# Joining the MLP stage and the second attention stage of a four-stage kernel into one program

## The reference, cut to what matters

```python
x = x + _layernorm(_L0_attn_ref(_layernorm(x), ...))   # attention with a running maximum
x = x + _layernorm(_L0_ffn_ref(_layernorm(x), ...))    # the MLP
x = x + _layernorm(_L1_attn_ref(_layernorm(x), ...))   # spectral attention
x = x + _layernorm(_L1_ffn_ref(_layernorm(x), ...))    # experts, one chosen per token

def _L0_ffn_ref(x, ...):                               # ternary weights, 128 -> 512 -> 512 -> 512 -> 128
    h = silu(_tlin(x, w1_w, w1_s)) * _tlin(x, w2_w, w2_s)
    h = gelu(_tlin(h, h1_w, h1_s)); h = gelu(_tlin(h, h2_w, h2_s))
    return _tlin(h, w3_w, w3_s)

def _L1_attn_ref(x, w_qkv, w_out):                     # 8 heads of 16 features
    q, k, v = split(x @ w_qkv)
    kv = cumsum(fft(k) * fft(v), axis=1)
    return ifft(kv * conj(fft(q))).real @ w_out
```

## Time and profile before

| what | value |
|---|---|
| runs, us | 1738.9, 1739.12, 1739.66 (median 1739.12) |
| the profiled execution's own time, us | 1737.36 |
| its span, first to last instruction, us | 1735.6 |
| PE busy | 1554.0 us, 90% of the span |
| DVE busy | 1288.1 us, 74% |
| ACT busy | 1164.1 us, 67% |
| POOL busy | 713.0 us, 41% |
| mean granted PE clock | 0.948 of full speed |

### The profile page before, as it was taken

How to read it: one execution, slowest core, us unless ns; L and a number is a source line. 1 busy time by engine, 2 the same in 40 slices (tenths; PEclk the granted TensorE clock), 3 DMA queues, 4 the chain that set the end, 5 groups by cost and what they waited for, 6 DMA issues and landing times. The chain is left out here.

```text
span 1735.6 us, 34433 instructions
## 1 busy us (share of the span) xinstructions
PE 1554.0 (90%) x8456; PEld 851.6 (49%) x8456; DVE 1288.1 (74%) x3545; ACT 1164.1 (67%) x2434; POOL 713.0 (41%) x1011
## 2 busy tenths in 40 slices
PE   4999999999999999999669999999949997896995
PEld 2333333333333333333247777777725655564773
DVE  4899999999999999999646666666636885323664
ACT  1588888888888888888646666667614455563663
POOL 2224433434443434333332333333314442474886
PEclk7799999999999999999879999999979998998998
DMA  4223223323222232331000000000030000444442
GB/s 124 61 78 93 82 85 94 91 75 90 82 86 86 80 98 84 108 91 45 8 7 1 1 1 0 0 0 0 1 102 1 1 1 1 137 154 130 140 136 67
DMA packets 83617, 109.24 MB, mean 63 GB/s; under 512 B 15915, under 2 KB 48945, under 8 KB 83520
## 3 DMA queue, kind: packets, MB, share of 16 engines
q1 hardware_dynamic: 77120, 91.28, 18.6%
q0 software_dynamic: 6400, 16.82, 2.7%
HBM read 63.24 MB, written 40.08 MB: 60 GB/s over the span
## 5 line engine op out<-in xcount | busy, mean ns | idle before, releaser
L838 DVE TENSOR_REDUCE bmax<-PS 128x8 f32<-128x512 f32 x1024 | 651.1, 683 | 60.0 <-PE PS L576 57.7
L688 ACT ACTIVATE EX<-PS 128x512 f32<-128x512 f32 x1024 | 564.0, 603 | 102.9 <-PE PS L587 93.6
L576 PE MATMUL PS<-KR,QR 33*128 33x512 f32 x1024 | 408.3, 468 | 37.9 <-DVE bmax L838 24.9
L587 PE MATMUL PS<-QR,KR 64*128 64x512 f32 x1024 | 395.9, 459 | 1.6 <-ACT EX L688 1.5
L576 PEld LDWEIGHTS PS<-KR,QR 33*128 33x128 f32 x1024 | 166.3, 188 | 350.8 <-DVE bmax L838 295.9
L597 PE MATMUL PS<-EX,VS 128*9 128x512 f32 x2048 | 268.6, 596 | 1.2 <-ACT EX L688 1.2
L587 PEld LDWEIGHTS PS<-QR,KR 64*128 64x128 f32 x1024 | 161.6, 185 | 11.3 <-ACT EX L688 10.2
L1030 PE MATMUL PS<-pA,wb 128*128 128x512 f32 x640 | 156.9, 401 | 0.0
L773 POOL TENSOR_TENSOR m_diff<-m_prev,m_all 128x16 f32<-128x16 f32 x64 | 14.3, 223 | 311.5 <-DVE m_all L850 311.5
L1030 PEld LDWEIGHTS PS<-pA,wb 128*128 128x128 f32 x640 | 120.1, 191 | 27.5
L1178 ACT ACTIVATE gelud<-PS,scales 128x512 f32<-128x512 f32 x128 | 88.4, 690 | 61.3 <-PE PS L1030 58.2
(11 more groups left out here) (230 smaller groups left out, 2784.4 us busy)
## 6 DMA issues: line engine op xcount, KB each, us to landing
QR<-q_scr SPq DMA_DIRECT2D x256, 64.0 KB, 2.4
KR<-k_scr SPq DMA_DIRECT2D x256, 64.0 KB, 2.3
big<-row_scr SPq DMA_DIRECT2D x72, 192.5 KB, 2.4
k_scr<-partsB SPq DMA_DIRECT2D x42, 256.0 KB, 2.9
q_scr<-partsB SPq DMA_DIRECT2D x28, 256.0 KB, 3.0
X<-in_L_attn_x SPq DMA_DIRECT2D x16, 256.0 KB, 3.0
X<-x SPq DMA_DIRECT2D x16, 256.0 KB, 2.4
xB<-in_L_attn_x SPq DMA_DIRECT2D x14, 256.0 KB, 3.3
```

The lines of the kernel that those rows point to most:

```text
L576: pe.matmul(PS[:, bank_of(i, n), :], QR[rows, i, h // 2, t * P:(t + 1) * P], KR[rows, i, h // 2, :], start=True, stop=True).then_inc(tile_ ...
L587: pe.matmul(PS[:, RING3 + bank_of(j, n), :], KR[rows, j, h // 2, kt * P:(kt + 1) * P], QR[rows, j, h // 2, :], start=True, stop=True).then ...
L688: act.activation(EX[:, n % (2 * HG), :], PS[:, RING3 + bank_of(j, n), :], ACT.Exp, scale=SCALE).then_inc(ex_set, 1)
L838: dve.tensor_reduce(bmax[:, i % 2, n, :], PS[:, bank_of(i, n), :].rearrange("p (b k) -> p b k", k=BLK), AX_X, ALU.max).then_inc(tile_max, 1)
```

## The change

The MLP's block is dissolved. Its engine programs become functions (`mlp_sync`, `mlp_tensor`, ...) that are called at the head of the second attention's block, so there is no barrier between the two.

- `run_pairs` no longer runs the drain. Each engine writes it out behind its last pair, and a part of it moves behind the first instructions of the attention: `turn` of chunks 14 and 15 behind `combine(0)` and `output(0)` on PE, `copy_xT` likewise on ACT, `x_stats` and `x_rows` of chunk 15 behind `products(0)` and `products(1)` on DVE.
- SP loads the fold matrices once the last first-layer product is done (`in_done`), into a part of the buffer `row` that lies where `pX` lay; `row` itself is used much later. The two matrices of `combine` get a buffer of their own, `mix`, and are loaded with `gate_w` and the constants after the MLP's last product (`mlp_done`). `w6_in` now counts seven transfers, `w5_in` still four.
- New waits keep banks and buffers apart: `xT3_set` before a chunk's `project`, `lnB["steps"]` before the first q products and the first `combine`, `xT3_set` before the first `output` and the first `logits`, `hi_set` before the folds, `mlp_done` before DVE's constants.
- PE's last `turn_y` stands behind the If and the Else, so the jump over the Else side now lies between `layer_out` and `turn_y` of chunk 15.

The diff without changes of indentation, cut:

```diff
@@ run_pairs
             step(PAIRS - 1, True, True)
-            step(PAIRS, False, True)
@@ end of the MLP's PE program
                 with pe.If(exact == 1):
                     run_pairs(pe, step_of(True))
+                turn_y(PAIRS - 1, 0)
+                layer_out(PAIRS - 1, 1, True)
                 with pe.Else():
                     run_pairs(pe, step_of(False))
+                turn_y(PAIRS - 1, 0)
+                layer_out(PAIRS - 1, 1, False)
+            turn_y(PAIRS - 1, 1)
+            return turn
@@ end of the MLP's POOL and ACT programs
                 run_pairs(pool, step)
+            step(PAIRS, False, True)
...
                 run_pairs(act, step)
+            copy_y(PAIRS - 1, 0)
+            copy_y(PAIRS - 1, 1)
+            return copy_xT
@@ end of the MLP's DVE program
                 run_pairs(dve, step)
+            y_stats(PAIRS - 1, 0)
+            y_rows(PAIRS - 1, 0)
+            x_stats(PAIRS - 1, 0)
+            y_stats(PAIRS - 1, 1)
+            x_rows(PAIRS - 1, 0)
+            y_rows(PAIRS - 1, 1)
+            return x_stats, x_rows
@@ buffers of the attention
+        mix = sb("mix", [P, 2, P])
+        row = sb("row", [P, 2, NT, ROW])
+        early = row[:].rearrange("p s t r -> p (s t r)")
+        wqkvT = early[:, 0:3 * P].rearrange("p (k i) -> p k i", k=3)
+        wout1 = early[:, 3 * P:4 * P]
+        turns = early[:, 4 * P:8 * P].rearrange("p (k i) -> p k i", k=4)
@@ SP
-                sp.dma_start(wqkvT[:], ...).then_inc(w5_in, 16)
-                sp.dma_start(wout1[:], io["L1_attn_w_out"]).then_inc(w5_in, 16)
-                sp.dma_start(dft[:], ...).then_inc(w5_in, 16)
-                sp.dma_start(gate_w[:], io["L1_ffn_gate_w"]).then_inc(w5_in, 16)
+                mlp_sync(sp)
+                sp.wait_ge(in_done, PAIRS * 16)
+                sp.dma_start(wqkvT, ...).then_inc(w5_in, 16)
+                sp.dma_start(wout1, io["L1_attn_w_out"]).then_inc(w5_in, 16)
+                sp.dma_start(turns[:, 0:2, :], ...).then_inc(w5_in, 16)
+                sp.dma_start(turns[:, 2:4, :], ...).then_inc(w5_in, 16)
+                sp.wait_ge(mlp_done, 2 * PAIRS)
+                sp.dma_start(mix[:], ...).then_inc(w6_in, 16)
+                sp.dma_start(gate_w[:], io["L1_ffn_gate_w"]).then_inc(w6_in, 16)
@@ PE
+                turn_x4 = mlp_tensor(pe)
                 pe.wait_ge(w5_in, 64)
+                pe.wait_ge(hi_set, PAIRS * 16)
...
                 def project(c, s):
                     xT = chunk_of(XT, c)
+                    pe.wait_ge(xT3_set, c + 1)
...
                     if late(c, 1):
                         pe.wait_ge(qq_set, c)
+                    else:
+                        pe.wait_ge(lnB["steps"], (NCH - 1) * LN_SPLIT)
...
                 def combine(c, s):
...
+                    else:
+                        pe.wait_ge(w6_in, 112)
+                        pe.wait_ge(lnB["steps"], NCH * LN_SPLIT)
...
                 run_stages(pe, NCH, [(0, project), (6, ranks), (4, turn), (1, combine), (2, output), (5, logits),
+                                     (1, lambda c, s: turn_x4(PAIRS - 1, 0) if c == 0 else None),
+                                     (2, lambda c, s: turn_x4(PAIRS - 1, 1) if c == 0 else None),
                                      (SHARED_LAG, shared)])
@@ ACT
+                copy_x4 = mlp_scalar(act)
...
-                act.wait_ge(w6_in, 80)
+                act.wait_ge(w6_in, 112)
...
+                                      (1, lambda c, s: copy_x4(PAIRS - 1, 0) if c == 0 else None),
+                                      (2, lambda c, s: copy_x4(PAIRS - 1, 1) if c == 0 else None),
@@ DVE
+                x4_stats, x4_rows = mlp_vector(dve)
+                dve.wait_ge(mlp_done, 2 * PAIRS)
                 dve.memset(ones5[:], 1.0).then_inc(const5_set, 1)
...
-                dve.wait_ge(w6_in, 80)
+                dve.wait_ge(w6_in, 112)
...
-                run_stages(dve, NCH, [(0, products), (3, residual), ...
+                run_stages(dve, NCH, [(0, products), (0, lambda c, s: x4_stats(PAIRS - 1, 1) if c == 0 else None),
+                                      (1, lambda c, s: x4_rows(PAIRS - 1, 1) if c == 0 else None), (3, residual), ...
```

More of the change, by code:

```diff
@@ L1195, in step @@
+                        turn_y(p - 1, 0)
+                        layer_out(p - 1, 1, exact)
+                    if now:
+                        layer_in(p, 1, exact)
                     if before:
-                        copy_y(p - 1, 0)
+                        turn_y(p - 1, 1)
                     if now:
-                        for n in range(2 * FB):
-                            silu(p, n)
-                            if n == FB and before:
-                                copy_y(p - 1, 1)
```

537 lines of the change are left out of this document (267 added, 270 removed).

## The result

The changed kernel took 1705.18 us, median of five runs (1703.78 to 1710.11), against 1739.12 before: a ratio of 0.9815, 95% interval 0.9802 to 0.9828. The forecast was 1716.4 with a range of 1713.0 to 1721.0. The direction was right and the time fell out of the range, on the fast side.

The account below looks back on a forecast made before the run. One chain of waits across engines, then on PE, was taken to bound the seam up to DVE's fourth `products`. 23.9 us less 1.2 gave 22.7: 1737.36 profiled becomes 1714.7, plus 1.76 gives 1716.4, range 1713.0 to 1721.0.

Parts of the forecast that it names:

- The step that failed: End of the MLP: its last product stays at 1260.13 us, as the pairs are the same code.
- clock in the folds: Seven folds after the last `turn_y`: run at the full clock, 1.7 us in place of 3.4.
- two groups of transposes on PE: Two groups of four transposes moved into the attention: 0.66 us each, about 0.6 counting, 1.2 in all, hidden by nothing.
- gain at the fourth `products`: Sum at the start of the second attention: 23.9 us less 1.2 for transposes, 22.7; v(3) ends at 1289.8 instead of 1312.46.
- The jump: PE's jump over the Else side ahead of the last `turn_y`: `turn_y` begins between 1260.9 and 1262.7, late end taken.
- a covered jump: Bound for PE's jump wholly covered by the last products in its queue: gain 23.1 us, time 1716.0.
- The constants: DVE sets its constants behind the last `y_rows`: 1.2 us, so `products(0)` starts at 1271.4.
- ids: Seven `w6_in` transfers land at 1267.7; ACT copies k and q until about 1269.8, PE needs more at 1270.4: covered.
- the clock didn't stay low: Rival: half clock persists into the attention, 7 us more per chunk; 1758 if for six chunks; chance 3%.
- the first rival: Clock falls once in the drain: folds take 3.4 us instead of 1.7, gain 20.7, time 1718.4; chance 13%.
- The rival without overlap: A wait ties the first projection to the drain's end; only pause and loads go: 12.3 us, 1726.8; chance 10%.
- a microsecond or two either way: Bound for clock holes behind 1300 us falling differently against the work: a microsecond or two.

Follow-up runs that it names:

- wb_off_64: Changed kernel with pads putting `wb` back at 32 modulo 64 and the other buffers at multiples of 64, distance `wb` to `pB` 96: 1714.95 us, ratio 0.9868.
- operands_moved: Changed kernel with `wb` kept and `pX`, `yv`, `pA`, `pB` moved by 64 bytes, distance `wb` to `pB` 128: 1714.44 us, ratio 0.9861.
- no_jump: Changed kernel with only the MLP's exact path on PE, no branch and no other path: ratio 0.9807 to before, seam 29.72 us against 29.71.
- drain_first: Changed kernel with the whole drain of the last half ahead of the folds again, early loads kept: ratio 0.9894 to before, seam 42.97 us.
- late_loads: Changed kernel with the fold matrices loaded only behind the last MLP product: ratio 0.9829 to before, seam 34.68 us.
- wb_on_128: Kernel before with `wb` moved by 96 bytes and `pX`, `pA`, `pB` by 256, distance `wb` to `pB` 0: 1726.23 us, ratio 0.9934.
- gap_filled: Changed kernel with seven unread products ahead of the wait for the previous pair's gate in every first layer but the first: 1701.07 us, ratio 0.9786.
- drain_first_late_loads: Changed kernel with the whole drain ahead of the folds and fold matrices loaded after the last MLP product: ratio 0.9895 to before, seam 42.95 us.

## Why the prediction was off

**The step that failed** is the first of the walk: "the last product, 1260.13, which nothing of the change moves: the MLP's pairs are the same code". The code was the same, the buffers' places were not. In place of 1260.13 the last product came at 1253.55, behind a stage 7.0 us shorter. With the places' effect undone, the changed kernel takes 1714.95 (wb_off_64) and 1714.44 us (operands_moved), both in the range and 1.5 to 2.0 us from the forecast. So of the miss of 11.2 us some 8 to 10 come from the places (0.9868 and 0.9861 against 0.9815, times 1739, give 9.2 and 8.0; the medians 9.8 and 9.3), and the rest is within what runs scatter. How the places make it is in two parts. Directly: among the kernels without dips, the one with blocks of 15.04 and 15.10 takes 367.1 us for the stage, the one with 14.82 362.8, so 4.3 us. The remainder through dips of 1.57 us, of which faster products leave fewer; for executions without a profile that is an inference.

The miss can be split another way. The profiled execution was to take 1714.7 and took 1710.11: 6.6 us less from the last product, 2.0 more behind the seam. The other 6.6 us of the miss stand in the step from the profiled execution to the median, for which the prediction added 1.76, as before, where after the median lies 4.93 below. The mean granted clocks suggest why: 0.953 in the profiled execution, 0.955 to 0.958 in the other four. One dip of 3.4 us at 0.50 takes 0.001 off the mean over 1708 us, so the 0.003 between the profiled execution and the median one (0.956) would be three dips, or 4.7 us. That is an estimate; the mean doesn't say where the clock was low.

**The seam**, term by term, in us after the last product, predicted and measured:

| term | predicted | measured |
|---|---|---|
| `turn_y` starts, behind the jump | 2.6 | 1.45 |
| clock in the folds | 1.00 | 1.00 |
| first projection | 6.0 | 4.66 |
| end of the last `y_rows` | 10.0 | 10.06 |
| constants on DVE | 1.2 | 1.5 |
| `products(0)` | 11.3 | 11.60 |
| `combine(0)` | 14.6 | 14.77 |
| two groups of transposes on PE | 1.2 in all | 0.44 each |
| gain at the fourth `products` | 22.7 | 22.71 |

- *The jump* was mis-sized (1.8 of delay taken, 0.67 measured), and it did not matter for the sum: DVE's queue sets `products(0)`, and the folds have slack. The prediction's own walk says so, with PE ready at 1270.4 and DVE at 1271.4. So its aside that a covered jump would bring 23.1 did not follow from it, and no_jump brought nothing.
- *The constants* took 0.3 more, since the cast of `trib` took 0.83 us here, against 0.23. It ran beside POOL's addition into `X` (1263.69 to 1264.96) and ended 0.08 us behind it. In the eight profiles where that addition is under way the cast takes 0.83 us; in all others, where it isn't, 0.17 to 0.23, so in drain_first:

```profile
1268.20 0.17 DVE L1877 CAST trib<-tri 128x128 bf16<-128x128 f32 x1
```

Transfers don't explain it: before, the cast took 0.23 us at 1288.21, and in the microsecond from 1289 they moved 219 GB/s. The transposes took 0.3 less. The exact hit of the sum owes something to such errors of opposite sign.
- *ids*: ACT's copy of k waited 2.07 us for them and still ran beside PE's products. Covered, as said.
- *The rivals*: the clock didn't fall, the overlap came about, the clock didn't stay low. But drain_first and late_loads show how near the first rival was, and that the reason against it was weak. The prediction read the fall at 1265.7, 4.1 us after PE's last work; the window's mean of 0.70 puts it at 1265.4, so 3.8. And it is no measure of what a pause may last: in late_loads the clock fell 0.8 us into PE's wait, behind a stretch of little work, and in the pairs waits of 2 us were enough. The rival without overlap was priced at a gain of 12.3; drain_first, which comes nearest to it, keeps 9.4 of the seam.
- *Behind the seam* 425.0 us pass after, 423.0 before (span less the fourth `products`). The 2 us were allowed for ("a microsecond or two either way"). Of them 1.7 lie between the first and the last of the 64 indexed transfers into `row_scr` (94.8 us before, 96.5 after); in the other profiles of the first group of runs the whole stretch takes 422.4 to 425.1.

What stays open: why the time of a product follows the distance of its operands, and whether fewer dips are what puts the median after 4.9 us below the profiled execution; the other four have no profile.

## What to carry to other kernels

"The same code" isn't the same time when buffers move: before forecasting a stage as untouched, compare the addresses of its operands in both programs, above all of weights and moving operands in a row of reloading products. A change that adds or reorders buffers should be timed with pads that keep the old distance, or its gain is credited to the wrong cause. And at a seam, find the queue that the first shared instruction stands in (here DVE's constants) before pricing waits on the other engines.

## What the runs showed of the hardware

- Products on fp32r operands of 128x512 with a weight load each step by 229 ns (14.67 / 64) when weights and moving operand lie 0 modulo 256 bytes apart, by 231 (14.81) at 64, and by 235 to 236 at the other distances seen; over 1408 of them, with the dips that go with it, 0 in place of 96 is worth 13 us of 1739 in the kernel before (wb_on_128).
- Seven useless products in a wait of 2 us at the head of each pair made the kernel 3.8 us faster, since they kept the granted clock at 1.00 through the MLP (gap_filled).
- The same late transfers cost nothing when PE waits for something else (drain_first_late_loads) and 5 us when it doesn't, 1.2 of them by the halved clock in one group of ten small products alone (late_loads).
- A cast on DVE of 128x128 float32 to bf16 takes 0.17 to 0.23 us, and 0.83 us when POOL's addition of two 128x512 tiles is under way (eight profiles).
